# Aggregating edge messages by runs of ten edges on VectorE, and then four products per group on TensorE in place of twenty

## The reference

```
h   = relu(layernorm(x))
z   = [h[senders], h[receivers], edge] @ [W1 | Wa1] + [b1 | ba1]      # 128 columns per edge
msg = silu(z[:, :64]) @ W2 + b2
att = softmax over all edges of (silu(z[:, 64:]) @ Wa2 + ba2)
agg[n] = sum of msg * att over the edges whose receiver is n
out = x + silu([h, agg] @ Wu1 + bu1) @ Wu2 + bu2
```

## Time and profile before

| | |
|---|---|
| median of 3 runs | 2107.86 us (2105.93 to 2108.01) |
| the profiled execution, first to last instruction (its span) | 2482.0 us |
| its time outside the span | the page gives none |
| busy share of the span | PE 44%, PEld 39%, DVE 44%, ACT 37%, POOL 62% |
| mean granted TensorE clock | 0.668 |
| DMA | 228.43 MB, mean 92 GB/s |

### The profile page before, as it was taken

The page is one execution under the profiler, slowest core; times in us unless marked ns, Lnnn a source line. Parts: engine busy times, 40 slices in busy tenths (PEclk is TensorE's granted clock), DMA queues, the critical chain, the costliest instruction groups (busy, mean ns, idle before and its releaser), DMA issues.

```text
span 2482.0 us, 21022 instructions
## 1 busy us (share of the span) xinstructions
PE 1101.1 (44%) x6767; PEld 963.4 (39%) x6767; DVE 1086.6 (44%) x2367; ACT 919.5 (37%) x1107; POOL 1529.9 (62%) x1628
## 2 busy tenths in 40 slices
PE   4334444444444444444444444444444444444447
PEld 3223343444333333444333334343433333444444
DVE  4344444444444444444444444444444444444445
ACT  3333333334333333334333333343433333333433
POOL 4666666666666666666666666666666666666650
PEclk8566666666666666666666666666666666666766
DMA  7433333333333333333333333333333333333321
GB/s 202 106 90 90 90 89 88 92 91 95 98 93 88 90 88 88 90 93 90 99 95 89 89 90 89 87 94 89 98 95 91 89 90 90 87 93 90 95 65 27
DMA packets 101990, 228.43 MB, mean 92 GB/s; under 512 B 45184, under 2 KB 65460, under 8 KB 91636
## 3 DMA queue, kind: packets, MB, share of 16 engines
q1 hardware_dynamic: 47588, 120.63, 18.5%
q0 software_dynamic: 51584, 105.75, 17.2%
q10 hardware_dynamic: 2704, 0.66, 0.1%
HBM read 218.91 MB, written 8.00 MB: 91 GB/s over the span
## 4 chain that ended last, share of the span: by engine, by line
issue 48%; PE 33%; DVE 9%; another core or an unknown queue 7%; ACT 1%; SPq 1%; DVEq 0%; DMA 0%; ACTq 0%
PE bank L622 20%; PE bank L636 11%; DVE hot L865 2%; DVE v L902 2%; DVE bank L912 1%; DVE prod L895 1%; PE bank L732 1%; PE bank L722 0%; DVE lgb L921 0%; DVEq L875 0%; ACT comb L492 0%; PE bank L584 0%; ACT s L524 0%; PE bank L655 0%
## 5 line engine op out<-in xcount | busy, mean ns | idle before, releaser
L404 POOL DMA_INDIRECT p_rows<-p_tab,src_all x1612 | 1521.9, 944 | 872.3 <-issue 464.7
L622 PE MATMUL bank<-q_win,comb 128*128 128x128 f32 x3224 | 723.7, 369 | 981.9 <-issue 963.8
L622 PEld LDWEIGHTS bank<-q_win,comb 128*128 128x128 f32 x3224 | 643.9, 279 | 1099.1 <-issue 1095.4
L492 ACT ACTIVATE comb<-dst_b,row_of 96x1024 f32<-96x1024 int32 (+1 forms) x162 | 219.0, 1352 | 1336.6 <-PE bank L622 1227.8
L911 DVE TENSOR_TENSOR bank<-bank,p_rows 128x128 f32<-128x128 f32 x80 | 23.9, 299 | 1205.5 <-remote 672.6
L636 PE MATMUL bank<-hot,v 128*65 128x96 f32 x3200 | 320.1, 252 | 344.7 <-issue 274.8
L636 PEld LDWEIGHTS bank<-hot,v 128*65 128x65 f32 x3200 | 282.7, 141 | 342.1 <-issue 264.5
L912 DVE TENSOR_TENSOR bank<-bank,p_rows 128x512 f32<-128x512 f32 (+1 forms) x403 | 266.5, 666 | 71.7 <-PE bank L622 38.6
L524 ACT ACTIVATE s<-bank 128x512 f32<-128x512 f32 x403 | 232.1, 589 | 108.7 <-DVE bank L912 83.8
L498 ACT ACTIVATE comb<-comb,ones 96x1024 f32<-96x1024 f32 (+1 forms) x162 | 218.9, 1351 | 2.7
L865 DVE TENSOR_TENSOR hot<-bank,rel 128x960 f32<-128x960 f32 x162 | 178.3, 1139 | 0.0
(11 more groups left out here) (108 smaller groups left out, 304.0 us busy)
## 6 DMA issues: line engine op xcount, KB each, us to landing
dst_b<-dst_row SPq DMA_DIRECT2D x80, 960.0 KB
p_rows<-p_tab,src_all POOLq DMA_INDIRECT x1612
comb<-efT SPq DMA_DIRECT2D x80, 320.0 KB
q_win<-q_tab SPq DMA_DIRECT2D x81, 48.0 KB
p_tab<-s SPq DMA_DIRECT2D x12, 256.0 KB
q_tab<-s SPq DMA_DIRECT2D x12, 256.0 KB
out<-s SPq DMA_DIRECT2D x6, 256.0 KB, 2.3
x_sb<-x SPq DMA_DIRECT2D x2, 512.0 KB, 5.1
```

The source lines that it names most:

```text
L404: pool.indirect_dma_start(p_rows[:, a, t * H2:(t + 1) * H2], None, p_tab, bass.IndirectOffsetOnAxis(src_all[:, g * TG + t:g * TG + t + 1], ...
L492: nc.scalar.activation(comb[0:WIN, a, c0:c1], dst_b[:, c0:c1], ACT.Abs, bias=row_of[0:WIN, bass.ds(g, 1)]).then_inc(abs_ok, 1)
L622: last = nc.tensor.matmul(ps_z[q][:, (t % TQ) * H2:(t % TQ + 1) * H2], comb[:, a, t * P:(t + 1) * P], q_win[:, a, :], start=True, stop=True)
```

## The change

A group's edges are laid out anew on the host: partition p holds the 20 consecutive edges 20p to 20p+19 (in the last group 12) instead of every 128th. The 20 edges of a partition are two runs of ten. Since the edges are sorted and each node has more edges than a run, a run touches at most two receivers: the one of its first edge and the one of its last. VectorE forms two weighted copies of the messages, one with the weights of the edges that belong to the run's first node and one with those of the other edges, and adds each up over the ten edges. This leaves four rows of 65 per partition (`run_sum`), and TensorE multiplies these four with four one-hots in place of twenty.

```
-                nc.vector.tensor_tensor(hot[:, t0 * WIN:(t0 + n) * WIN]...            # twice, n = 10 tiles
+                nc.vector.tensor_tensor(hot[:].rearrange("p (r k n) -> p r k n", r=RUNS, k=2), ...   # once, 4 x 96

+            def segment_sums(g, a):
+                T = tiles(g)
+                n = T // RUNS
+                here = slice(g * TG, g * TG + T)
+                att = s2[:, a, 0:T, U1:2 * U1]
+                nc.vector.tensor_tensor(w_run[:, 0, 0:T], ps_w[:, 0:T], first_run[:, here], ALU.mult)
+                nc.vector.scalar_tensor_tensor(w_run[:, 1, 0:T], first_run[:, here], 0.5, ps_w[:, 0:T], ALU.is_lt, ALU.mult)
+                for k, weighed in ((0, att), (1, v[:, 0:T, :])):
+                    dve.wait_ge(w_run_ok, 2 * g + 1 + k)
+                    nc.vector.tensor_tensor(weighed, s2[:, a, 0:T, 0:U1], w_run[:, k, 0:T]...broadcast, ALU.mult)
+                for k, weighed in ((0, att), (1, v[:, 0:T, :])):
+                    dve.wait_ge(v_ok, 2 * g + 1 + k)
+                    nc.vector.tensor_reduce(run_sum[:, k::2, :], weighed.rearrange("p (r t) u -> p r u t", r=RUNS), AX.X, ALU.add)

-                weigh(T, a, a).then_inc(v_ok, 1)
+                nc.vector.tensor_reduce(wsum[:, a:a + 1], ps_w[:, 0:T], AX.X, ALU.add)
+                segment_sums(g, a)

-                for t in range(T):
-                    last = nc.tensor.matmul(ps_part[0:U1, 0:WIN], v[:, t, :], hot[:, t * WIN:(t + 1) * WIN], ...)
+                for i in range(SEGS):
+                    last = nc.tensor.matmul(ps_part[0:U1, 0:WIN], run_sum[:, i, :], hot[:, i * WIN:(i + 1) * WIN], ...)
```

More of the change, by code:

```diff
@@ L126, in build @@
         p_rows = sb("p_rows", [P, 2, TG * H2])
-        hot = sb("hot", [P, TG * WIN])
+        first_run = sb("first_run", [P, C // P])
+        fits = sb("fits", [P, C // P])
+        hot = sb("hot", [P, SEGS * WIN])
+        w_run = sb("w_run", [P, 2, TG])
+        run_sum = sb("run_sum", [P, SEGS, U1])
         comb = sb("comb", [P, 2, TG * P])
@@ L257, in tiles, with runs @@
             return TL if is_last(g) else TG
+        def runs(t, g):
+            return t[:, g * TG:g * TG + tiles(g)].rearrange("p (r t) -> p r t", r=RUNS)
         def per(a, g, n):
@@ L664, in _ @@
                 own_part(b)
[L665 to L674, removed]
+            pe.wait_ge(zp_ok, 1)
+            nc.tensor.matmul(ps_zall, ones[:], zp[:], start=True, stop=True).then_inc(zall_done, 1)
+            sums(LAST)
             pe.wait_ge(flag_ok, 1)
@@ L852, in worst_fit @@
                 chain(nc.vector.tensor_scalar(bad[:, 0:1], bad[:, 0:1], float(1 - WIN), None, ALU.add))
-                nc.vector.scalar_tensor_tensor(bad[:, 2:3], bad[:, 1:2], -1.0, bad[:, 0:1], ALU.mult, ALU.max).then_inc(bad_ok, 1)
+                chain(nc.vector.scalar_tensor_tensor(bad[:, 2:3], bad[:, 1:2], -1.0, bad[:, 0:1], ALU.mult, ALU.max))
+                for lo, hi, n in ((0, LAST * TG, TG // RUNS), (LAST * TG, C // P, TL // RUNS)):
+                    of_run = rel[:, lo:hi].rearrange("p (r t) -> p r t", t=n)
+                    for keep, end in ((first_run, 0), (fits, n - 1)):
+                        nc.vector.tensor_tensor(keep[:, lo:hi].rearrange("p (r t) -> p r t", t=n), of_run,
+                                                of_run[:, :, end:end + 1].broadcast_to([P, (hi - lo) // n, n]), ALU.is_equal).then_inc(run_fit, 1)
+                dve.wait_ge(run_fit, 4)
+                chain(nc.vector.tensor_tensor(fits[:], fits[:], first_run[:], ALU.max))
+                chain(nc.vector.tensor_reduce(bad[:, 0:1], fits[:], AX.X, ALU.min))
+                chain(nc.vector.tensor_scalar(bad[:, 0:1], bad[:, 0:1], -1.0, 1.0, ALU.mult, ALU.add))
+                nc.vector.tensor_tensor(bad[:, 2:3], bad[:, 2:3], bad[:, 0:1], ALU.max).then_inc(bad_ok, 1)
             def set_flag():
@@ L859, in set_flag, with one_hots @@
                 nc.vector.tensor_scalar(flag[:], bad1[:, 2:3], 0.0, None, ALU.is_gt).then_inc(flag_ok, 1)
[L861 to L867, removed]
+            def one_hots(g):
+                n = tiles(g) // RUNS
+                nc.vector.tensor_tensor(hot[:].rearrange("p (r k n) -> p r k n", r=RUNS, k=2),
+                                        iota_c[:, 0:WIN].unsqueeze(1).unsqueeze(1).broadcast_to([P, RUNS, 2, WIN]),
+                                        runs(rel, g)[:, :, 0::n - 1].unsqueeze(3).broadcast_to([P, RUNS, 2, WIN]), ALU.is_equal).then_inc(hot_ok, 1)
             def set_ref(g, node):
@@ L972, in group @@
                 if late:
-                    one_hots(g - 1, 0)
-                    one_hots(g - 1, 1)
+                    one_hots(g - 1)
                     weighted(g - 1, 1 - a)
@@ L1022, in _ @@
             add_part(LAST - 1, 1, node_before)
-            one_hots(LAST, 0)
+            one_hots(LAST)
             dve.wait_ge(ref_ok, 2 * LAST)
@@ L1028, in _ @@
             dve.wait_ge(wm_ok, 1)
-            nc.vector.tensor_tensor(v[:, 0:TL, :], s2[:, 0, 0:TL, 0:U1], ps_w[:, 0:TL].unsqueeze(2).broadcast_to([P, TL, U1]), ALU.mult).then_inc(v_ok, 1)
-            one_hots(LAST, 1)
             nc.vector.tensor_reduce(wsum[:, 0:1], ps_w[:, 0:TL], AX.X, ALU.add).then_inc(ws_ok, 1)
@@ L1142 @@
     last = -(-(N_EDGES - full) // (4 * P)) * 4 * P
-    edges = np.concatenate([np.arange(full), np.arange(N_EDGES - last, N_EDGES)])
+    edges = np.concatenate([np.arange(full).reshape(-1, P, EDGE_TILES).transpose(0, 2, 1).reshape(-1),
+                            np.arange(N_EDGES - last, N_EDGES).reshape(P, -1).T.reshape(-1)])
     src, dst, ef = (np.ascontiguousarray(inputs[n])[edges] for n in ("src", "dst", "edge_attr_32"))
```

28 lines of the change are left out of this document (18 added, 10 removed).

## The result

The changed kernel takes 2209.89 us (2206.11 to 2212.3, 4 runs), the kernel before 2106.89: a ratio of 1.0501 [1.0469, 1.0533], 103 us slower. The prediction was 2251 with a range of 2110 to 2315.

What follows compares the result with a forecast made beforehand. GpSimd's chain of gathers was taken to bound the kernel. To 2107.9 us came 134 for held gathers, 3.6 for `worst_fit` and 5.6 for the end: 2251 us, range 2110 to 2315.

Steps and rivals of the forecast that it cites:

- What bounds the kernel: Whole kernel: GpSimd's chain of 1,612 gathers at 1.248 us, 2012 us, bounds the ordinary run with hardly a gap.
- the gap between 2482 and 2107: Profiled span against median: 351 us of GpSimd waits and 32 of tail, said to belong to the execution with the profiler.
- the profile's span fell by more than 200 us: Sign in the changed kernel's profile: its span falls by about 200 us or more, to near the ordinary time.
- GpSimd's waits for VectorE vanished: Sign in the changed kernel's profile: these waits all but vanish and GpSimd's busy share rises over 70%.
- TensorE, no gain: TensorE's 16 fewer products per group save 645 us busy in the whole kernel, hidden altogether beside the gathers.
- VectorE per group, +3.4 us: VectorE's work per group: +5.06 for products and reductions, -1.66 for one-hots; hidden as time except in the last group.
- The hold, 1.7 us per group: New VectorE products with both inputs in SBUF hold up gathers: 1.7 us in 79 groups, 134 us, bounds 24 and 229.
- `worst_fit`, 3.6 us: Once: three long VectorE instructions with both inputs in SBUF hold up gathers by about 1.2 us each, +3.6 (0 to 5.5).
- The end, 5.6 us: After the last gather: VectorE's +3.4 us in full, then +2.2 us in the chain up to TensorE's last products.
- No blocking (2114): Rival: products like the new ones leave gathers alone, only the longer end is left, 2114 us; chance 0.13.
- TensorE as a bound: Rival: TensorE's issue also bounds the ordinary run, so fewer products bring the time to 2100 us; chance 0.05.
- VectorE did not become the bound: Rival: strided reductions many times slower, at 7.5 us each, make VectorE the bound, 2436 us; chance 0.03.

Runs made afterwards that it cites:

- e4: The kernel before, with TensorE carrying out the 20 products of every group except the last twice: 2108.74 us, ratio 1.0017 to the kernel before.
- e11: The changed kernel as it is, run again where the kernel before takes about 2450 us: 2439.33 us, ratio 0.9954 to the kernel before.
- e7: Changed kernel with `w_run` in PSUM, its products also writing [run, column, edge] so the reductions read neighbours: 2473.73 us, ratio 1.0083 to the kernel before.
- e3: The changed kernel with each of its two products cut in four pieces of 5 tiles, all inputs in SBUF: 2121.34 us, ratio 1.0086 to the kernel before.
- e10: The changed kernel with the first product's weights in PSUM, the second's in SBUF: 2457.46 us, ratio 1.0014 to the kernel before.
- e2: The kernel before with its weights `ps_w` in SBUF instead of PSUM: 2197.98 us, ratio 1.0439 to the kernel before.
- e1: The changed kernel with `w_run`, second input of the two new products, in PSUM instead of SBUF: 2118.39 us, ratio 1.0064 to the kernel before.

## Why the prediction was right

**What bounds the kernel.** Right for the measured runs, and the step that the rest hangs on: 1,612 gathers at 1.248 us, with nothing between them, confirmed by e4. Its reason for the gap between 2482 and 2107 was wrong. I put it down to the profiler; e4's profiled execution shows none of it, and the later runs show the same slowness without it. By the sum of the gathers the median came out right all the same. Two of the prediction's signs came true by luck: the profile's span fell by more than 200 us (to 2206.3), and GpSimd's waits for VectorE vanished. Both come from the first condition, in which this profile was taken: e4, without the change, spans 2101.9 us and has 0.6 us of such waits. In the second one (e11) the changed kernel spans 2434.3 us and 225 us of waits remain, and the change costs nothing (0.9954).

**TensorE, no gain.** Right: it is busy 690.4 us instead of 1101.1 (how much of the fall the other condition makes is not known), and the time did not fall with it. The trap was the earlier trace rows: waits that are long and true, in a condition that the timed runs were not in.

**VectorE per group, +3.4 us.** Too low. 1477.5 - 1101.9 (e4) is 375.6 us over 81 groups, 4.6 us each. The one-hots (546 ns), the small products (160 ns) and the long ones were as priced; the term that failed is the reductions, 2.43 and 2.54 us instead of 1.51, for the stride (e7). They alone are 1.95 us more; that only 1.2 of it shows is in part the overlap of neighbouring records, which busy time counts once. As the prediction said, in the groups this is hidden: 18 us of work in a group of 26.

**The hold, 1.7 us per group.** The mechanism was right: which operands, and the 0.82 us that remain. One detail was not: it is not a step 0.12 us after the gather's start that meets the product (e3). The size was the one left open between 1.1 (the gather gets in between the two products) and 2.3 (they hold it together). I took the middle; it is the first, 1.18 per group, and the two long gathers per group show it. This one term, 134 us taken against 95, is nearly the whole error of the forecast: 2251 - 39 = 2212, measured 2210. That 1.18 is so close to the mean of 1.1 is luck. The mean holds for a start anywhere, but the products meet the gathers at nearly the same moment in most groups, and I had that moment wrong by 0.4 us: the first product starts 3.7 us after the end of the group's last gather, not 3.3. At other moments the same kind of product costs 0.6 per group (e10) or 1.2 (e2). The page "SBUF — State Buffer" of the Trainium skill (section "Who interferes with whom") says that a VectorE instruction with two SBUF inputs contends with a GpSimd instruction that reads SBUF, and these runs agree. Its inference that `tensor_tensor` doesn't stall descriptor generation doesn't carry over to this indirect gather: e1 and e2 measure 95 and 97 us.

**`worst_fit`, 3.6 us.** Right. In e1, where the other holds are gone, three gathers beside its long comparisons take 2.53, 1.44 and 1.73 us: 2.9 us over normal, and the gathers' sum is 3.4 over e4's.

**The end, 5.6 us.** Right in its sum, in part by luck: from the end of the last gather to the end of the span 55.2 us against 49.3 in e4, +5.9. The last rows of the changed kernel (before: the earlier trace rows):

```profile
2148.83 2.25 POOL L414 DMA_INDIRECT p_rows<-p_tab,src_all  x1 [0.30 <-issue]
...
2165.07 0.17 DVE L1056 TENSOR_TENSOR bank<-bank,mask 128x12 f32<-128x12 f32 x1
...
2170.73 1.51 PE L649 MATMUL bank<-hot,run_sum 128*65 128x96 f32 x8 [4.59 <-DVE run_sum L932]
...
2175.52 2.08 PE L668 MATMUL bank<-hP,wu1d 128*128 128x512 f32 x2 [3.27 <-issue]
...
2177.53 3.69 PE L728 MATMUL bank<-acc,wws 65*64 65x512 f32 x8
```

From the mask to the first L728 it is 12.46 us, where the earlier trace rows has 8.96: 3.5 longer, not 2.4 (the forecast's 2.2 and the 0.2 that the mask comes earlier), for the slow reductions and the slower eight matmuls. In e1, where no such hold moves the last gather, the end is 7.0 us longer than e4's; in the changed kernel the last gather is itself held by 1.3 us, which hides some of it.

**The sum**: 98.2 (gathers, 1620.5 - 1522.3) + 5.9 (end) + 0.3 (first gather) = 104.4, the difference of the two spans 2206.3 and 2101.9.

**The rivals.** No blocking (2114) is what e1 measures once the cause is taken away: 2118. TensorE as a bound is refuted for the timed condition (e4). For the other it was not tested: the change gains 0.5% there, and e4 was not run in it. VectorE did not become the bound.

No version here beats the kernel before where it takes 2107 us: even e1 pays for the longer end, and there is nothing to win while 1,612 gathers at 1.248 us fill 2012 of them.

## What to carry to other kernels

Before pricing a saving, add up the strictly regular queue and compare it with the timed median: if it alone explains the time, the waits of a profile that is longer than the median need not be those of the timed runs. Where GpSimd issues gathers, look at where both inputs of every long VectorE product lie; moving one of them to PSUM was worth 92 us here, and a weight moved the other way cost 92. If both must be in SBUF, cut the product into short pieces (quarters took 2121 us in place of 2210). Placing it so that it ends just after a gather has started should help as well; that follows from the rule, and no run tried it on purpose.

## What the runs showed of the hardware

- A gather of 128 rows takes 0.944 us and 0.30 to the next. A VectorE product with two SBUF inputs under way at its start lengthens it to that product's end + 0.82 us (795 gathers, within 0.02 us), except for most that start in the product's first 0.045 us (49 of 52 not held). One that starts up to 0.25 us after the gather did nothing in 79 cases and held it to its end in all eight of e2. Single holds by products of 1.5 us were 0.16 to 1.59 us, by the moment; by products of 0.83 us up to 0.56, of 0.49 us up to 0.34.
- A VectorE reduction of 1,300 elements takes 1.49 us when it reads neighbours and 2.43 or 2.54 at strides of 260 or 520 bytes; a product takes 1.50 and, writing at a stride of 40 bytes, 2.48.
- The same kernel takes 2106 or 2452 us. In the second condition TensorE's instructions come 0.7 or 1.4 us apart for long stretches, as in the earlier trace rows. What causes it, no run shows; a difference between chips is not excluded.
